# Sorting two halves of the tokens into 39 expert blocks instead of 46, in a four-layer kernel on one core

## The reference

```python
# layer 0: per sample one expert of 8: LN(gelu(x @ Wi[e] + bi) @ Wo[e] + bo + x)
# layer 1, per sample a FiLM with constants of its subject, then top 2 of 8 experts for each token:
h = h_norm * gamma[:, None, :] + beta[:, None, :]
probs = softmax(h_flat @ router_w)
gates, idx = top_k(probs, 2);  gates = gates / gates.sum(-1, keepdims=True)
hid = relu(einsum('nd,edf->nef', h_flat, exp_w1) + exp_b1)      # 128 -> 512
eout = einsum('nef,efd->ned', hid, exp_w2) + exp_b2             # 512 -> 128
x = x + sum over the two chosen experts of gate * eout
# layer 2: a rotation of feature pairs by theta and phi of the sample
# layer 3: per sample an adapter 128 -> 32 -> gelu -> expert 32x32 -> 128, + residual, LayerNorm
```

## Time and profile before

| | |
|---|---|
| median of three runs | 227.44 us (225.57 to 227.86) |
| span of the profiled execution | 242.6 us; its device time is not given apart from that |
| busy, share of the span | PE 188.6 us (78%), DVE 112.3 (46%), ACT 115.2 (47%), POOL 100.2 (41%) |
| chain that ended last | PE 56%, issue 13%, DVE 11%, ACT 7%, DMA 6% |
| its largest line | L789 (all matmuls) 51%; then the gather's DMA, 6% |
| gathers and fetches on POOL | 46 x 0.964 us and 32 x 0.967 us busy |

### The profile page before, as it was taken

The page is one execution under the profiler, slowest core; times in us unless marked ns, Lnnn a source line. Parts: engine busy times, 40 slices in busy tenths (PEclk is TensorE's granted clock), DMA queues, the critical chain, the costliest instruction groups (busy, mean ns, idle before and its releaser), DMA issues.

```text
span 242.6 us, 5805 instructions
## 1 busy us (share of the span) xinstructions
PE 188.6 (78%) x1390; PEld 172.2 (71%) x1390; DVE 112.3 (46%) x556; ACT 115.2 (47%) x370; POOL 100.2 (41%) x115
## 2 busy tenths in 40 slices
PE   6999988899399599897967777978989973164760
PEld 6999978899389499786956667977879962143440
DVE  6226696788816504383114233111403534605775
ACT  3645855664145454674524554466464820302241
POOL 4136143114842613334266565666623207772000
PEclk9999997997759759997999999999999998555555
DMA  6999999993713433656564646767653431311001
GB/s 201 292 304 300 330 312 274 248 282 107 220 35 101 146 82 86 182 168 179 131 140 121 176 128 143 206 157 203 186 143 94 127 86 45 96 49 30 22 22 43
DMA packets 40474, 37.60 MB, mean 155 GB/s; under 512 B 4481, under 2 KB 31003, under 8 KB 40443
## 3 DMA queue, kind: packets, MB, share of 16 engines
q1 hardware_dynamic: 33419, 29.32, 42.7%
q0 software_dynamic: 2496, 5.12, 9.7%
q10 hardware_dynamic: 4528, 2.81, 3.8%
HBM read 32.11 MB, written 5.11 MB: 153 GB/s over the span
## 4 chain that ended last, share of the span: by engine, by line
PE 56%; issue 13%; DVE 11%; ACT 7%; DMA 6%; another core or an unknown queue 3%; POOL 2%; ACTq 1%; DVEq 0%; POOLq 0%
PE bank L789 51%; DMA got<-h_rows,src_i 6%; ACT hid L708 3%; PE bank L954 3%; DVE st L1154 1%; ACT zg L731 1%; ACT gotT L698 1%; POOL got L495 1%; POOL rstd L480 1%; PE bank L800 1%; DVE zg L1443 1%; ACT xT L716 1%; PE bank L981 1%; DVE st L1390 1%
## 5 line engine op out<-in xcount | busy, mean ns | idle before, releaser
L708 ACT ACTIVATE hid<-bank,small 128x128 f32<-128x128 f32 x184 | 52.5, 374 | 42.4 <-PE bank L789 41.0
L495 POOL DMA_INDIRECT got<-h_rows,src_i x46 | 44.4, 964 | 43.1 <-PE bank L789 25.2
L789 PE MATMUL bank<-gotT,w_now 128*128 128x128 f32 x368 | 55.0, 297 | 7.1 <-issue 6.2
L789 PEld LDWEIGHTS bank<-gotT,w_now 128*128 128x128 f32 x368 | 49.3, 208 | 10.6 <-issue 9.2
L789 PE MATMUL bank<-w,hid 128*128 x368 | 50.9, 284 | 0.0
L1365 DVE TENSOR_TENSOR y_blk<-bank,b_tab 128x128 f32<-128x128 f32 x46 | 13.3, 289 | 74.3 <-PE bank L789 61.5
L789 PEld LDWEIGHTS bank<-w,hid 128*128 128x128 f32 x368 | 47.0, 200 | 0.1
L506 POOL DMA_INDIRECT w_place<-slot_rows,slot_i x32 | 30.9, 967 | 33.3 <-PE bank L954 16.6
L954 PE MATMUL bank<-ident,got 128*128 128x128 f32 x46 | 14.1, 307 | 14.8 <-DMA got<-h_rows,src_i 9.8
L650 ACT ACTIVATE act<-bank,small 128x128 f32<-128x128 f32 x64 | 18.3, 369 | 13.6 <-PE bank L789 13.6
L698 ACT ACTIVATE gotT<-bank 128x128 f32<-128x128 f32 x46 | 13.3, 289 | 20.5 <-PE bank L954 8.8
(11 more groups left out here) (206 smaller groups left out, 252.6 us busy)
## 6 DMA issues: line engine op xcount, KB each, us to landing
w_now<-in_exp_w SPq DMA_DIRECT2D x46, 256.0 KB
w_place<-in_l_wi SPq DMA_DIRECT2D x16, 256.0 KB, 5.4
w_place<-in_l_wo SPq DMA_DIRECT2D x16, 256.0 KB, 5.9
slot_rows<-y_blk SPq DMA_DIRECT2D x46, 64.0 KB
rows<-in_l_rows SPq DMA_DIRECT2D x16, 128.0 KB, 5.0
w<-in_exp_w SPq DMA_DIRECT2D x8, 256.0 KB, 5.7
x_sb<-in_x ACTq DMA_DIRECT2D x4, 256.0 KB, 5.1
h_rows<-h_row ACTq DMA_DIRECT2D x4, 256.0 KB, 3.3
```

Of the source, the lines that this page charges most:

```text
L495: g_.indirect_dma_start(got[:, n % RING, :], None, h_dram[n // BL], bass.IndirectOffsetOnAxis(ap=src_i[:, n:n + 1], axis=0))\
L708: last = a_.activation(hid[:, n % HRING, c, :], up_bank(n)[:, c * P:(c + 1) * P], ACT.Relu, bias=cols[:, bass.ds(e * FC + (R_B1 + c), 1)])
L789: return t_.matmul(out_, lhsT, rhs, start=start, stop=stop)
```

## The change

Both halves now share one table of blocks: `NBLK = (4096 + 8*127)//128 = 39`. The first half fills only whole blocks ahead of time, at least `EARLY = 9`; what is left over of each of its experts joins the second half's rows of that expert in the other 30. A slot of the first half is stored by block 22 at the latest (`SETTLED = 23`). The second half's index is needed from block 9 on. Its sort moves into steps 1 to 8 on all engines. New DVE operations (`later_bases`, `more_blocks`, `part_experts`, `late_experts`) place the leftovers. The sums are fetched one token tile at a time in the order of the units. Layer 3 runs in eight units of two samples: four inside the loop from block 30 on (`BEGIN3`), four behind it, with their PE order written out; the last unit is normalised on DVE (`last_norm`), with its root from POOL, where ACT's Sqrt stood.

```diff
-    NBLK = HALVES * BL
+    NBLK = (TOPK * NB * S + E1 * (P - 1)) // P
+    EARLY = -((E1 * (P - 1) - TOPK * HB * S) // P)
+    LATE = NBLK - EARLY
+    SETTLED = (TOPK * HB * S + E1 * (P - 1)) // P
-    RING, YRING, TRING, WRING, HRING = 16, 4, 4, 6, 3
-    LEAD = AHEAD + 2
+    RING, YRING, TRING, WRING, HRING = 16, 12, 4, 6, 3
+    HELD = 4
-    UNITS = [(GS * g, GS) for g in range(HG)] + [(b, 2) for b in range(GS * HG, NB, 2)]
+    US = 2
+    UNITS = [(b, US) for b in range(0, NB, US)]
+    HU = HB // US
+    BEGIN3 = 30
...
# POOL
-            for n in range(BL):
-                if n >= LEAD:
-                    beside_up(n - LEAD)
...
+            for n in range(EARLY):
                 gather(n)
...
+            hot_tiles(1)
+            hot_tiles(2)
+            pool.wait_ge(v_idx, 2)
...
+            for n in range(EARLY, EARLY + HELD):
+                gather(n)
+            first_half = [row_ for u in range(HU) for row_ in rows_of(u)]
+            for n in range(EARLY + HELD, NBLK):
+                pool.wait_ge(p_u, n - HELD + 1)
+                gather(n)
+                if n == SETTLED + HELD:
+                    pool.wait_ge(v_slot, 1)
+                    stored(SETTLED)
+                if n >= SETTLED + HELD:
+                    fetch_row(*first_half.pop(0))
+            for row_ in first_half:
+                fetch_row(*row_)
+            pool.wait_ge(v_slot, 2)
+            stored(NBLK)
+            for u in range(HU, NU):
+                for row_ in rows_of(u):
+                    fetch_row(*row_)
...
# PE
+                if k == EARLY:
+                    down_of(k - 2)
+                    inverse(2)
+                    down_of(k - 1)
                     pe.wait_ge(v_exp, 2)
...
+                    rows_T(k)
+                    rows_T(k + 1)
                 if k < NBLK:
                     blk_up(k)
...
-                if k == 14:
-                    inverse(1, 0, KT // 2)
-                if k == 15:
-                    inverse(1, KT // 2, KT)
+                if k == 7:
+                    inverse(1)
...
+            l3_T(HU)
+            l3_T(HU + 1)
+            l3_down(HU)
+            l3_residual(HU)
+            l3_T(HU + 2)
+            l3_up(HU)
...
# DVE, beside the blocks
+                if k == 4:
                     top2(2)
-                if s == 8:
                     top2(3)
-                if s == 10:
-                    count_blocks(1)
...
+                if k == 5:
+                    ranks(1)
+                    more_blocks()
                     sort_slots(1)
-                    hot_blocks(1)
-                if 12 <= s < 14:
-                    hot_slots(8 * (s - 12), 8 * (s - 11))
+                    hot_blocks(2)
+                    hot_slots(1, 0, KT)
...
-                if s == 16:
+                if k == 8:
                     sources(1)
...
+            def more_blocks():
+                do(v_.tensor_tensor(more[:], held[:], run[:, :, HB - 1], ALU.add))
+                settle()
+                do(v_.tensor_scalar(more[:], more[:], float(P - 1) - (P - 1) / 2, 1.0 / P, ALU.add, ALU.mult))
...
+            def last_norm(u):
+                before = ch.n
+                for k in unit(u):
...
```

More of the change, by code:

```diff
@@ L326, in conditional_layers_kernel @@
         v_o3 = sem("v_o3")
+        g_o3 = sem("g_o3")
         class Chain:
@@ L358, in conditional_layers_kernel @@
         y_bank = lambda n: bank[3 + n % 2][:, 0:D]
+        at_once = lambda n: (n in (0, 1) or EARLY <= n < EARLY + 2)
+        rows_of_step = lambda k: [n for n in ((2, 3) if k == 0 else (EARLY + 2, EARLY + 3) if k == EARLY else (k + 3,))
+                                  if (n < EARLY or k >= EARLY) and n < NBLK]
         got_bank = bank[0][:, 0:P]
@@ L562, in _ @@
                     power(1, 3)
+                if n == 6:
+                    power(2, 2)
                 if n == 7:
-                    power(2, 2)
-                if n == 8:
                     power(2, 3)
[L567 to L586, removed]
-            power3(0)
-            stored(1)
-            for u in range(2, NU):
-                fetch(u)
+            hot_tiles(1)
+            hot_tiles(2)
+            pool.wait_ge(v_idx, 2)
+            pool.wait_ge(st_h[2], 16)
+            pool.wait_ge(st_h[3], 16)
+            for n in range(EARLY, EARLY + HELD):
[16 more added lines that the diff above has]
+                    fetch_row(*row_)
+            power3(HU)
+            power3(HU + 1)
+            gain_shift3(HU)
+            power3(HU + 2)
+            gain_shift3(HU + 1)
+            power3(HU + 3)
+            gain_shift3(HU + 2)
         @block.scalar
@@ L1557, in _ @@
-            stats3(NU - 1)
-            shift_of_norm3(NU - 1)
-            scale_shift3(NU - 2)
-            scale_shift3(NU - 1)
+                if 17 <= k < 21:
+                    rotations(4 * (k - 17), 4 * (k - 16))
+                if 21 <= k < 24:
+                    down_rotated(k - 21)
+                u, odd = divmod(k - BEGIN3 + 2, 2)
+                if 0 <= u < HU and odd == 0:
+                    combine(u, unit(u))
+                if 2 <= u < HU + 2 and odd == 0:
+                    stats3(u - 2)
+                    shift_of_norm3(u - 2)
@@ new lines, in _ @@
+                if 3 <= u < HU + 3 and odd == 1 and k < NBLK:
+                    scale_shift3(u - 3)
+            scale_shift3(HU - 2)
+            scale_shift3(HU - 1)
+            combine(HU, unit(HU))
+            combine(HU + 1, unit(HU + 1))
+            combine(HU + 2, unit(HU + 2))
+            stats3(HU)
+            combine(HU + 3, unit(HU + 3))
+            shift_of_norm3(HU)
+            stats3(HU + 1)
+            shift_of_norm3(HU + 1)
+            stats3(HU + 2)
+            shift_of_norm3(HU + 2)
@@ L1564 @@
+            stats3(HU + 3)
+            last_norm(HU + 3)
 def kernel(**inputs):
```

530 lines of the change are left out of this document (284 added, 246 removed).

## The result

The changed kernel takes 250.44 us (median of four runs, 246.59 to 252.62) against 227.02 of the kernel before: ratio 1.0997, 95% interval 1.0871 to 1.1124. Ratios here compare the fast executions of a kernel alone (of these four 246.59 and 249.57), so they aren't the quotients of the medians, and the profiled execution, 251.3 us, isn't one of them. Measured again later it was 251.61, ratio 1.1147 (1.1051 to 1.1242). The direction was forecast; the size, 233.5 with a range up to 241, was far too small.

A forecast was written before the change was run, and what follows sets the result against it. The kernel before was taken as bound by PE in the loop, behind layer 0, and by a serial tail. Up(9) at 106.0, the loop to 192.7, first fetch at 195.1 and tail 38.4 gave 233.5 us, range 219 to 241.

The forecast's parts named there:

- the bubble: At block 9 PE waits for the second half's sort; up(9) at 106, eating 4.5 of the seven blocks removed.
- leash: From gather 13 POOL waits for up(n-4), was up(n-5): 2.28 us per block, up to 2.73 with longer arrival.
- the hole at the stores: Gather 28 waits for block 22's store, so PE stands 4.8 us once, before up(26).
- the stall at unit 2: In the loop, PE waits for unit 2's fetched rows in step 34: about 3.6 us, between nothing and 5.
- Fetches and layer 3 in the loop: 2.58 us a block from gather 28, 2.95 from block 30, plus about 3.6 stall for unit 2's rows.
- the last up, three downs and the add: End of the loop, from up(38) to the end of the last add: 4.3 us.
- The tail is worth nothing: From the first of 16 fetches to the end: 38.4 us against 37.2 before, one us either way.
- 5.5 (estimate): End of the tail: statistics, power, last_norm and the store, 5.5 us.
- late wakes: ACT starting late behind PE's ups, with PE idle 16.4 us in loop and tail; read as the profiled execution's only.
- A: Rival, faster: late wakes belong to every run and the changed kernel escapes them, 218.3; 217 to 224, chance 0.22.
- B: Rival, no change: 4.4 us lie around every launch, or the leash doesn't bind; 224 to 229.7, chance 0.27.
- C: Rival, worse: longer arrivals or weight loads set the pace to 2.73, giving 241; 237 to 246, chance 0.14.

The follow-up runs named there:

- e3: The changed kernel with gathers 13 to 26 waiting for the up eight blocks back in place of four: 247.07 us.
- e7: The changed kernel with the last four units of layer 3 one after the other on PE, ACT's and DVE's lists to match: 247.21 us, ratio 1.1022.
- e4: The changed kernel with statistics and Newton roots of units 2 and 3 moved on DVE behind the last block's add: 248.92 us, ratio 1.1074.
- e9: The changed kernel with leash eight, load before store, later store wait and layer 3, serial tail, earlier second inverse, and DVE's last adds and tail reordered: 220.93 us.
- e12: The kernel of e9 with POOL done after the powers of units 4 and 5, the later work moved to DVE: 218.44 us, ratio 0.9665.
- e5: The changed kernel with SP's weight load ahead of the store in its list, the leash still four: 250.75 us, ratio 1.1186.
- e6: The changed kernel with both edits, gathers 13 to 26 waiting eight blocks back and the weight load ahead of the store: 246.17 us, ratio 1.0967.
- e1: The kernel before, unchanged, profiled once more: 224.37 us, span 222.6.

## Why the prediction was wrong, step by step

From the sum (233.5) to the span (249.6) it is 16.1 us, and the predicted stations can be read off the rows:

| step | predicted, us | measured, us | missed |
|---|---|---|---|
| up(9), the bubble | 106.0 | 107.95 | 1.9 |
| up(9) to up(25), restart and leash | 37.8 | 39.3 | 1.5 |
| up(25) to up(26), the stores | 7.1 | 7.1 | 0.0 |
| up(26) to up(30), fetch and gather | 10.3 | 11.5 | 1.2 |
| up(30) to up(38), layer 3 | 27.2 | 31.4 | 4.2 |
| up(38) to the first of 16 fetches | 6.7 | 11.1 | 4.4 |
| tail | 38.4 | 41.3 | 2.9 |

The table is of one execution. In e3 to e7, whose edits don't touch the sort, up(9) stands at 103.3 to 105.0, earlier than forecast and not later; up(30) to up(38) takes 31.1 to 33.5 in them, up(38) to the first fetch, but for e4, 11.1 to 11.5, and the tail, but for e7, 41.1 to 41.3. So the large misses that every execution shows are those of the last three rows, 11.5 us of the 16.1 here.

The mechanisms were right: bubble, pace, the hole at the stores, the stall at unit 2 are all where they were put, and in this execution the first four terms hold within 2 us each. In the first, luck helped. The second half's index, forecast for 102.2, stood at 102.37 + 0.19 = 102.6 here and at 98.46 + 0.19 = 98.7 in e7; but from gather 9 to up(9) it took 107.95 - 102.83 = 5.1 us here and 104.35 - 98.92 = 5.4 in e7, where the sum had 3.5, as PE's list has the transpose of gather 10, too, ahead of up(9).

- **What failed first is "Fetches and layer 3 in the loop".** It costed PE and POOL and gave DVE nothing. But a unit's statistics and Newton root take 194.89 - 191.59 = 3.3 us of DVE's list in the changed kernel, in front of the adds that the stores wait for. The last add came 205.58 - 197.23 = 8.4 us behind the start of the last up, where "the last up, three downs and the add" allowed 4.3. e4 shows that 2.7 of it are the two roots that it moved. What is left there, 5.6, is PE's: its list has the up of unit 3 among the last downs. In e9, with no unit of layer 3 there and no root on DVE, the last add is at 176.13, 3.9 behind up(38) (172.19). So about 4 is what the place costs with nothing else in it.
- **Every hole costs more than itself.** The sum had one restart at half clock, 1.3. The windows of the changed kernel show the granted clock behind each hole:

```profile
107.00:115.00 8.00, 6.15 (x28) 5.56 (x28) 0.00 (x0) 3.34 (x13) 2.49 (x3) 0.50 0.36 103
115.00:148.00 33.00, 29.43 (x240) 27.63 (x240) 11.53 (x34) 21.06 (x74) 12.44 (x13) 0.98 0.53 158
148.00:154.00 6.00, 1.18 (x11) 0.98 (x9) 0.42 (x2) 1.14 (x4) 3.35 (x4) 0.96 0.53 141
154.00:158.00 4.00, 3.96 (x23) 3.96 (x24) 0.29 (x1) 1.70 (x6) 2.62 (x4) 0.63 0.20 44
185.00:190.00 5.00, 4.48 (x21) 4.13 (x22) 3.98 (x22) 1.33 (x4) 2.31 (x3) 0.50 0.15 42
```

  Behind the holes before 107, 154 and 185 PE runs at 0.50 to 0.63, the lower of its two levels for all or part of the stretch, and an up takes 1.92 in place of 1.06. Behind the stall of unit 2 the step up(35) to up(36) took 191.45 - 185.97 = 5.5 us against 2.95 in the sum. That is more than half of the 4.2 in this execution; in e3 to e7 the same step took 4.4 to 5.5, and the row missed 3.9 to 6.3. What the rest is, no run settled (1.07 us of "issue" ahead of unit 0's up at 175.28, where the list has two value loads, is a likely part).
- **"The tail is worth nothing" was wrong by 2.9.** Up to the last matmul the terms hold: 18.9 for the fetches, 2.6 for the last rows, 1.0 to the transposes, 9.4 to the end of the last up (230.81 to 240.21), together 31.9 against 32.9. What failed is "5.5 (estimate)" for the end: it took 249.6 - 240.21 = 9.4, and 3.3 of that is POOL's drain behind SP's close (249.4 against 246.1), which moving the last units' work to POOL put on the path (e12). The hand-written order, which was taken to be worth about nothing, costs 4.8 (e7).
- **The leash** was right at 2.3 to 2.4, but the weight load, which I gave "nothing below the pace", is a second loop of the same length (e3, e5, e6). The sum was right by it; the remedy would not have been.
- **The base was 3.6 too slow.** I took the profiled execution without its late wakes, 226.2, for the kernel before; its span in e1 is 222.6, and the 3.6 are those of up(9), 95.35 against 91.73. So the bubble eats not 4.5 of the seven blocks but about five: at the 103.3 to 105.0 of e3 to e7 the kernel before, by e1, is in block 13 or 14, with some 32 still ahead of it, and the changed one has 30. In the execution of the table, at 107.95, it is six. 7.3 + 16.1 + 3.6 = 27.0 is the whole distance of these two spans, 249.6 - 222.6; by the ratio 1.0997 it is some 22.5.

**The rivals.** A fell with e1: the late wakes are not in plain runs. The rule of the Trainium skill, page "Perfetto Trace Analysis", section "Tensor Engine Instruction (MATMUL, LD_WEIGHTS)", that a matmul's end is estimated, doesn't explain them: in e1 the same ends are 0.14 us from the wake. The 6.2 us of the Trainium skill, page "Runtime: NRT & Kernel Launch", section "The ~15µs preamble/postamble breakdown", which would put the reported time under the profile's total, are not seen here. The time is 1.7 us above the span in both kernels. B fell on that and on the pace: it needed 4.4 us around a launch, or 1.9 us a block in place of 2.38. C had the sign of the miss and not its cause: a gather that up(13) released took 123.58 - 119.97 = 3.6 to its transpose, within the bounds, and the pace stayed at 2.4. No rival named DVE, whose share of 46% in the page of the kernel before looked like room; in the changed kernel it had no pause over 0.6 us from 184.5 to 207.4.

## What to carry to other kernels

Seven blocks of work removed from the bound engine are worth little if the order that removes them needs its second input at block 9 in place of 23 (here about five of the seven went into that wait): before cutting work, ask when its inputs can be there. When work is moved beside a loop, add up every in-order engine of that stretch, also the one that the page shows half idle, and ask which loop-carried result stands behind the new work in its list. Where two loops of one length lie side by side, taking away either shows nothing; try both before dismissing one. And read a station off several executions: up(9) stood some 4 us apart in executions of the same code.

## What was not expected of the hardware

A profile can be of a disturbed execution: in the first one of the kernel before, ACT's relu started 1.3 to 2.4 us behind the modelled end of its up in many steps of a stretch of some 50 us, and its span was 20 us longer than that of the same program in e1. After holes of 2 to 5 us PE's granted clock was at its lower level again, 0.50 to 0.63 over the next 4 to 8 us. And POOL's closing drain took 6.65 us from the start of its last work in every kernel that gave it work at the end, 6.77 in e12, where nobody waited for it.
